# Attention projection of the last stage as three f32r products of high and low parts, with other shares of it moved into the aggregation stage

## The reference, cut to what matters

```
xn = layernorm(x)
x1 = x + gnn(xn, edges) @ W_up + linear_attention(xn) @ Wo + bo
out = x1 + ffn_fp4(layernorm(x1))        # gate, up, silu, down, each operand quantised
```

## Time and profile before

| | us |
|---|---|
| median of 3 runs (lowest, highest) | 1060.36 (1056.84, 1062.06) |
| the profiled execution | 1058.53 |
| its span in the trace | 1056.8 |
| aggregation (about 611 to 816) | 205 |
| last stage (816.2 to the end) | 240.6 |

### The profile page before, as it was taken

How to read it: one execution, slowest core, us unless ns; L and a number is a source line. 1 busy time by engine, 2 the same in 40 slices (tenths; PEclk the granted TensorE clock), 3 DMA queues, 4 the chain that set the end, 5 groups by cost and what they waited for, 6 DMA issues and landing times. The chain is left out here.

```text
span 1056.8 us, 17499 instructions
## 1 busy us (share of the span) xinstructions
PE 959.5 (91%) x5429; PEld 794.3 (75%) x5429; DVE 837.9 (79%) x1395; ACT 648.7 (61%) x1435; POOL 496.7 (47%) x582
## 2 busy tenths in 40 slices
PE   2698879999999999999997779999999879999986
PEld 2676779999999999999997357888898334454443
DVE  5875567888888888888888868998995768887776
ACT  3274446665765766666664568999898335554442
POOL 0211777777777777777771524444444200110000
PEclk9699889999999999999998899999999989999998
DMA  9304588989889898998872689989985364674314
GB/s 246 56 7 110 169 243 259 292 265 280 257 254 294 266 287 284 288 280 282 277 244 91 247 198 332 293 278 310 290 270 192 79 135 122 149 160 112 81 19 79
DMA packets 109977, 221.40 MB, mean 209 GB/s; under 512 B 25883, under 2 KB 58228, under 8 KB 109857
## 3 DMA queue, kind: packets, MB, share of 16 engines
q1 hardware_dynamic: 89053, 159.98, 47.2%
q0 software_dynamic: 20576, 60.08, 23.8%
q10 hardware_dynamic: 260, 0.20, 0.1%
HBM read 156.56 MB, written 62.95 MB: 208 GB/s over the span
## 5 line engine op out<-in xcount | busy, mean ns | idle before, releaser
L1024 POOL DMA_INDIRECT score_gath<-xl_rows,misc x324 | 347.4, 1072 | 101.6 <-issue 92.1
L1064 PE MATMUL score_ps_m<-x_hi,score_w_hi 128*128 128x416 f32 (+1 forms) x576 | 209.4, 363 | 2.1 <-DVE score_w_lo L1217 1.9
L1065 PE MATMUL score_ps_m<-x_lo,score_w_hi 128*128 128x416 f32 (+1 forms) x576 | 204.1, 354 | 0.0
L1066 PE MATMUL score_ps_m<-x_hi,score_w_lo 128*128 128x416 f32 (+1 forms) x576 | 204.1, 354 | 0.0
L1784 ACT ACTIVATE agg_gath<-agg_gath,prob 128x64 f32<-128x64 f32 x648 | 159.2, 353 | 6.7 <-DMA agg_gath<-edge_rows 6.4
L1196 DVE TENSOR_TENSOR score_zb<-score_gath,score_ps_x 128x1024 f32<-128x1024 f32 x81 | 98.8, 1219 | 67.6 <-PE score_ps_x L1047 57.9
L1733 PE MATMUL ps_all<-agg_gath,agg_hot 128*125 128x128 f32 x648 | 128.0, 280 | 9.8 <-DVE agg_hot L1839 6.4
L1735 PE MATMUL ps_all<-agg_gath,agg_hot 128*125 128x136 f32 x648 | 128.9, 281 | 0.0
L1733 PEld LDWEIGHTS ps_all<-agg_gath,agg_hot 128*125 128x125 f32 x648 | 100.5, 189 | 25.8 <-issue 25.2
L2081 PE MATMUL ps_all<-mix_w,phi_c 128*125 128x512 f32 x240 | 108.4, 602 | 5.8 <-DVEq L2355 5.2
L1064 PEld LDWEIGHTS score_ps_m<-x_hi,score_w_hi 128*128 128x128 f32 x576 | 109.7, 190 | 4.2 <-issue 2.6
(11 more groups left out here) (341 smaller groups left out, 1666.3 us busy)
## 6 DMA issues: line engine op xcount, KB each, us to landing
edge_rows<-score_gath SPq DMA_DIRECT2D x81, 528.0 KB, 3.8
agg_gath<-edge_rows SPq DMA_DIRECT2D x81, 528.0 KB, 5.6
local_bc<-local_rows SPq DMA_DIRECT2D x40, 224.0 KB
score_gath<-xl_rows,misc POOLq DMA_INDIRECT x324, 4.5
phi_c<-phi_rows SPq DMA_DIRECT2D x10, 500.0 KB, 6.1
x_bo<-in_x SPq DMA_DIRECT2D x10, 500.0 KB
x_bo<-in_L_mix_bo POOLq DMA_DIRECT2D x10, 500.0 KB, 7.2
out<-fin_x SPq DMA_DIRECT2D x9, 500.0 KB
```

The costliest lines, as they stand in the source:

```text
L1024: nc.gpsimd.indirect_dma_start(out=gath[:, g % GS, q, :], out_offset=None, in_=xl_rows, in_offset=bass.IndirectOffsetOnAxis(ap=src_idx[:, ...
L1064: pe.matmul(acc, w_hi[:, i % 2, kk, :], x_hi[:, kk, cols], start=(kk == 0), stop=False)
L1065: pe.matmul(acc, w_hi[:, i % 2, kk, :], x_lo[:, kk, cols], start=False, stop=False)
L1066: mm = pe.matmul(acc, w_lo[:, i % 2, kk, :], x_hi[:, kk, cols], start=False, stop=(kk == KC - 1))
```

## The change: what it does

The projection in `finish` is no longer f32 times f32. phi and `mix_w` are each split in a high part (rounded to f32r) and a low part (the rest, f32r), and each product becomes three f32r products: high x high, high x low, low x high. ACT makes the high parts (`split_high`, `high_phi`: a copy of 128 x 1024 for each panel, 128 x 750 or 1000 for each chunk), POOL subtracts to get the low parts (`split_low`, `low_phi`), in place over `mix_w` and `phi_c`. Panels 2, 3 and 4 are split by POOL alone during the aggregation, at groups 24, 32 and 40 (a copy and a subtraction each). Panels 5, 6 and 7 follow at the start of `finish`, panels 0 and 1 after `complete_x(2)`. `EARLY` changes from 4, 3, 3, 3, 3, 2, 2 to 8, 2, 2, 2, 2, 2, 2 panels for chunks 0 to 6: chunk 0's projection is done wholly in the aggregation, and `finish` has no `mix_part` for it. Tiles move to other places in memory.

```
-EARLY = [4, 3, 3, 3, 3, 2, 2] + [0] * (NC - 7)
+EARLY = [KC] + [2] * 6 + [0] * (NC - 7)
+PHI_O = 2
+SPLIT = [2, 3, 4, 5, 6, 7, 0, 1]
+SPLIT_EARLY = 3
+def split_low(nc, k, n):
+    kk = SPLIT[n]
+    nc.gpsimd.tensor_tensor(k.mix_lo[:, kk, :], k.mix_w[:, kk, :], k.mix_hi[kk][:, :].bitcast(F32),
+                            ALU.subtract).then_inc(k.s_mix_lo, 1)
...
 # aggregate, POOL
+                def split_early(n):
+                    kk = SPLIT[n]
+                    pool.wait_ge(s_piece, 2)
+                    nc.gpsimd.tensor_copy(k.mix_hi[kk][:, :], k.mix_w[:, kk, :]).then_inc(k.s_mix_hi, 1)
+                    pool.wait_ge(k.s_mix_hi, n + 1)
+                    split_low(nc, k, n)
                 for g in range(NG):
                     extras(g)
+                    for n in range(SPLIT_EARLY):
+                        if g == 24 + 8 * n:
+                            split_early(n)
...
 # finish, POOL
+                def low_phi(c):
+                    part = phi_c[:, c % 2, EARLY[c]:, :]
+                    pool.wait_ge(s_phi_hi, c)
+                    nc.gpsimd.tensor_tensor(phi_lo[:, c % 2, EARLY[c]:, :], part, phi_hi[:, c % 2, EARLY[c]:, :].bitcast(F32),
+                                            ALU.subtract).then_inc(s_phi_lo, 1)
+                low_phi(1)
+                for n in range(SPLIT_EARLY, 6):
+                    pool.wait_ge(k.s_mix_hi, n + 1)
+                    split_low(nc, k, n)
                 pool.wait_ge(k.s_own_in, 16 * 5)
...
                     x_add(nc, k, c, bias_rows(a))
+                    low_phi(c)
...
+                    if c == 0:
+                        for n in range(6, KC):
+                            pool.wait_ge(k.s_mix_hi, n + 1)
+                            split_low(nc, k, n)
...
 # finish, PE
                 def mix_part(c, half):
+                    if half == 0:
+                        pe.wait_ge(s_phi_lo, c)
                     for kk in range(EARLY[c], KC):
-                        pe.matmul(ps_y[0:C, half, :], phi_c[:, c % 2, kk, :], mix_w[:, kk, half * 512:half * 512 + 512],
-                                  start=(kk == EARLY[c]), stop=False)
+                        if half == 0:
+                            pe.wait_ge(k.s_mix_lo, SPLIT.index(kk) + 1)
+                        high, low = phi_hi[:, c % 2, kk, :], phi_lo[:, c % 2, kk, :]
+                        pe.matmul(ps_y[0:C, half, :], high, k.mix_hi[kk][:, cols], start=(kk == EARLY[c]), stop=False)
+                        pe.matmul(ps_y[0:C, half, :], high, k.mix_lo[:, kk, cols], start=False, stop=False)
+                        pe.matmul(ps_y[0:C, half, :], low, k.mix_hi[kk][:, cols], start=False, stop=False)
...
-                pe.wait_ge(s_phi[0], 16)
-                for half in range(2):
-                    mix_part(0, half)
                 turn_gnn(0)
...
 # finish, ACT
+                high_phi(1)
+                split_high(SPLIT_EARLY)
                 act.wait_ge(s_eps, 1)
                 act.wait_ge(s_den, 1)
                 act.activation(node[:, 2:4, :, :], node[:, 2:4, :, :], ACT.Exp).then_inc(s_pself, 1)
+                for n in range(SPLIT_EARLY + 1, 6):
+                    split_high(n)
                 for c in range(4):
                     copy_gnn(c)
...
                 copy_gnn(7)
+                for n in range(6, KC):
+                    split_high(n)
+                high_phi(2)
                 size_x(0)
...
                 normalise(1)
+                high_phi(3)
                 size_x(1)
...
                     gate(c - 1)
+                    if c + 2 < NC:
+                        high_phi(c + 2)
                     size_x(c)
```

More of the change, by code:

```diff
@@ L149, in allocate @@
     k.x_lo = nc.alloc_sbuf_tensor_at("x_lo", [P, KC, N], F32R, offset=x_at + 4 * KC * N)
+    k.mix_at = x_at
     k.mix_w = nc.alloc_sbuf_tensor_at("mix_w", [P, KC, D], F32, offset=x_at)
@@ L182, in allocate @@
     k.kv = sb("kv", [P, PANELS, P])
+    k.kv_at = at(k.kv, 4 * PANELS * P)
     misc = k.misc = sb("misc", [P, HID + 2 * PB * P])
@@ L199, in allocate_late @@
     k.agg_gath = ctx.enter_context(nc.sbuf_tensor("agg_gath", [P, AGG_SLOTS, GP, XW], F32))
+    gath_bytes = 4 * AGG_SLOTS * GP * XW
+    k.gath_at = nc.sbuf_base - gath_bytes
+    assert 4 * D * (KC - SPLIT_EARLY + 1) <= gath_bytes
+    k.s_mix_lo = ctx.enter_context(nc.semaphore("s_mix_lo"))
+    k.s_mix_hi = ctx.enter_context(nc.semaphore("s_mix_hi"))
+    homes = [k.parts_at, k.parts_at + 4 * D, k.kv_at] + [k.gath_at + 4 * D * n for n in range(KC - SPLIT_EARLY)]
+    k.mix_lo = nc.alloc_sbuf_tensor_at("mix_lo", [P, KC, D], F32R, offset=k.mix_at)
+    k.mix_hi = {kk: nc.alloc_sbuf_tensor_at(f"mix_hi{kk}", [P, D], F32R, offset=at) for kk, at in zip(SPLIT, homes)}
     k.prob = ctx.enter_context(nc.sbuf_tensor("prob", [P, PB * P, HEADS], F32))
@@ L210, in allocate_last @@
     k.phi_c = ctx.enter_context(nc.sbuf_tensor("phi_c", [P, 2, KC, C], F32))
+    k.phi_at = nc.sbuf_base - 8 * KC * C
     k.x_bo = ctx.enter_context(nc.sbuf_tensor("x_bo", [C, 2, D], F32))
@@ L1607, in aggregate @@
         hot = sb("hot", [P, OS, GP, C])
-        phi_o = sb("phi_o", [P, 5, 3, C])
+        phi_o = sb("phi_o", [P, 5, PHI_O, C])
         piece = sb("piece", [C, 512])
@@ L1669, in _ @@
                         for c in range(2, 7):
-                            sp.dma_start(phi_o[:, c - 2, :, :], k.phi_rows[0:3, :, C * c:C * c + C].rearrange("k p n -> p k n")).then_inc(s_phi_o, 16)
+                            sp.dma_start(phi_o[:, c - 2, :, :], k.phi_rows[0:PHI_O, :, C * c:C * c + C].rearrange("k p n -> p k n")).then_inc(s_phi_o, 16)
                     if g >= GS + 22 and (g - GS - 22) % 6 == 0 and (g - GS - 22) // 6 < 5:
@@ L1931, in sem @@
             return ctx.enter_context(nc.semaphore("fin_" + name))
-        h = k.kv[0:C, :, :].rearrange("p a b -> p (a b)")
-        square = k.parts[0:C, 0:D]
+        h = nc.alloc_sbuf_tensor_at("fin_h", [C, D], F32, offset=k.gath_at + 4 * D * (KC - SPLIT_EARLY))[:, :]
+        phi_hi = nc.alloc_sbuf_tensor_at("fin_phi_hi", [P, 2, KC, C], F32R, offset=k.parts_at + 8 * D)
+        phi_lo = nc.alloc_sbuf_tensor_at("fin_phi_lo", [P, 2, KC, C], F32R, offset=k.phi_at)
+        square = k.parts[0:C, 4 * D + D // 2:5 * D + D // 2]
         work = k.score[:, :, :].rearrange("p i h -> p (i h)")
-        coarse = k.parts[:, 3 * D:3 * D + D // 2].bitcast(BF16)
+        coarse = k.parts[:, 4 * D:4 * D + D // 2].bitcast(BF16)
         x1 = sb("x1", [C, 3, D])
@@ L1996, in finish @@
         s_tail = sem("s_tail")
+        s_phi_hi = sem("s_phi_hi")
+        s_phi_lo = sem("s_phi_lo")
         s_pself = sem("s_pself")
@@ L2079, in mix_part @@
                 def mix_part(c, half):
+                    cols = slice(half * 512, half * 512 + 512)
+                    if half == 0:
+                        pe.wait_ge(s_phi_lo, c)
                     for kk in range(EARLY[c], KC):
-                        pe.matmul(ps_y[0:C, half, :], phi_c[:, c % 2, kk, :], mix_w[:, kk, half * 512:half * 512 + 512],
-                                  start=(kk == EARLY[c]), stop=False)
+                        if half == 0:
[4 more added lines that the diff above has]
+                        pe.matmul(ps_y[0:C, half, :], low, k.mix_hi[kk][:, cols], start=False, stop=False)
                 def gnn_part(c, half):
@@ L2086, in gnn_part @@
                         m = pe.matmul(ps_y[0:C, half, :], gnn_t[:, kk, C * c:C * c + C], w_up[:, kk, half * 512:half * 512 + 512],
-                                      start=False, stop=(kk == 1))
+                                      start=(kk == 0 and EARLY[c] == KC), stop=(kk == 1))
                     if half:
@@ L2092, in projections @@
                     pe.wait_ge(s_x1, c)
-                    pe.wait_ge(s_phi[c % 2], 16 * (c // 2 + 1))
+                    mix_part(c, 0)
                     pe.wait_ge(s_gtc, c + 1)
-                    mix_part(c, 0)
                     if c in (1, 2):
@@ L2242, in _, with high_phi, split_high @@
                 act.activation(tail[:, :], ps_all[0:C, 5, 0:2 * HALF + UPPER], ACT.Copy).then_inc(s_tail, 1)
+                def high_phi(c):
+                    act.wait_ge(s_phi[c % 2], 16 * (c // 2 + 1))
+                    act.activation(phi_hi[:, c % 2, EARLY[c]:, :], phi_c[:, c % 2, EARLY[c]:, :], ACT.Copy).then_inc(s_phi_hi, 1)
+                def split_high(n):
+                    act.activation(k.mix_hi[SPLIT[n]][:, :], mix_w[:, SPLIT[n], :], ACT.Copy).then_inc(k.s_mix_hi, 1)
+                high_phi(1)
+                split_high(SPLIT_EARLY)
                 act.wait_ge(s_eps, 1)
```

## The result

The changed kernel takes 1080.49 us (median of 4 runs, 1079.93 to 1084.82), the kernel before beside it 1058.69 (4 runs, 1056.84 to 1062.06). The ratio is 1.0205, with a 95% interval of 1.0162 to 1.0248: slower by 22 us, inside the range, 3.5 us above the number forecast. The profiled execution took 1080.66 us, its span is 1078.9.

The account below looks back on a forecast made before the run. PE, ACT and DVE nearly full in the aggregation; in the last stage hand-overs, then DVE, then PE from 907.45. Terms 1.5 + 9.0 + 8.7 - 0.3 + 3.7 - 3.6 = +19.0 on 1058.5, said as 1077 us; range 1056 to 1088.

Parts of the forecast that it names:

- The mechanism: Each new POOL operation holds DVE operations with two SBUF inputs for its whole length, 1.9 to 2.55 us; chance 0.66.
- Rival 1: POOL does not hold DVE anywhere, so the kernel gets faster by 6 us, 1052 us; chance 0.12.
- Rival 2: POOL's hold on DVE never passes 0.52 us, ten times on 1052: 1057 us, the same; chance 0.08.
- The aggregation: POOL adds 11 us against DVE, partly taken by DVE's lead over PE: +1.5 us, bounds -2 and +8.
- rival 3: Aggregation takes POOL's 11 us nearly in full because DVE has no lead there: 1084 us; chance 0.14.
- Start and residual(1): Last stage: POOL's subtractions, ACT's high parts and PE's clock delay residual(0) by 9.0 us, then residual(1) by 8.7.
- the line through the earlier trace: POOL subtraction price from records of 256 and 384 columns: 2.55 us for 1024 columns, bounds 2.1 and 2.95.
- The clock's part: Start of last stage: PE, idle since the aggregation, loses 2.3 us on chunk 0's products at the lower clock level.
- ACT's 2.9: Before `size_x(0)`, on the way to residual(1): two `split_high` and `high_phi(2)` on ACT add 2.9 us.
- Iterations: After residual(2), POOL's `low_phi` makes DVE's 18.85 us 20.7, or 21.3 for 1000 columns: +3.7, then -3.6 us.
- ACT's `high_phi`: Iterations from 907.45 us: its cost counted as nothing; without that cover 0.8 to 1 us a chunk.
- The f32r products: Projection on PE: 0.232 us per 512-column product, bounds 0.19 and 0.232; period 20.5 us for chunks 7 to 9.

Follow-up runs that it names:

- experiment 6: Changed kernel with POOL's nine subtractions for phi's low part replaced by writes of zeros of the same shape: 1072.95 us, ratio 1.0152 to the kernel before.
- experiment 5: Changed kernel with the aggregation's three POOL subtractions cut to one column, its three copies kept whole: 1076.03 us, ratio 1.0165 to the kernel before.
- experiment 3: Kernel before with only the new shares of early panels (8, 2, 2, 2, 2, 2, 2), in f32, nothing split: 1063.64 us, ratio 1.0057.
- experiment 2: Changed kernel with only the aggregation's six POOL copies and subtractions cut to one column: 1072.52 us, ratio 1.0142 to the kernel before.
- experiment 1: Changed kernel with all its new POOL subtractions and copies cut to one column, PE and ACT work the same: 1053.17 us, ratio 0.995 to the kernel before.
- experiment 8: Same split as the change, but 16 early panels, ACT's high parts later where possible, every subtraction on POOL: 1069.12 us, ratio 1.0134 to the kernel before.

## Why the prediction was right

**The mechanism.** Right, and shown: POOL's operations hold DVE's, each DVE operation ends just behind POOL's, on both sides of the range of lengths (40 columns and 1024). But the prediction had it for DVE operations of two SBUF inputs alone, the only kind in the earlier trace rows, and in the iterations the operation held was nearly always L1931, which has one. That it is held for POOL's own time as well was not foreseen, so the price of an iteration came out right in part by luck. Rival 1, worked out at 1052, is the kernel with POOL's operations cut (1053). Rival 2, a hold of at most 0.52 us, fell at the first timeline: holds were 1.5 to 2.2 us. The Trainium skill (SBUF — State Buffer, Who interferes with whom) agrees with the rows: two SBUF inputs on DVE against a GpSimd read exclude each other for the whole instruction, and a GpSimd instruction that only writes does not hold them (0.20 and 0.19 us beside the write of experiment 6).

**The aggregation.** The step that failed: "DVE's lead over PE takes part of it", for which +1.5 was taken, with a bound of +8. It measured +9.2, beyond the bound. There was no lead to take it: six DVE operations are 8.8 us too long and PE's wait for `agg_hot` grows by 6.1. This is the mechanism of rival 3, which was given 0.14; its condition ("DVE has no lead there") held. The copy counts as well, 0.8 us each on DVE's records; with the copies alone 4.2 us of the aggregation stay (experiment 5). That the moved products cost nothing there was right (experiment 3: 206.05 against 205.9).

**Start and residual(1).** Right in kind, 1.0 and 1.6 us too long. A subtraction of 1024 columns made DVE's operations 2.0 to 2.2 us longer, not the 2.55 of the line through the earlier trace rows; POOL's records of 2.7 hold waits. The clock's part, 2.3 us for `gnn_part(0)`, measured 1.35 (4.80 against 3.45), and 1.1 to 2.6 in the other executions, so the 1.0 too long at the start is within what one execution differs from the next: with the same start residual(0) came 21.1 and 20.4 us into the stage in experiments 2 and 5. ACT's 2.9 measured 2.6.

**Iterations.** 20.7 was forecast and 20.5 measured for 750 columns, 21.3 and 20.9 to 21.35 for 1000. The five intervals from residual(4) were forecast at 105.1 and took 103.2, mostly because the last took 19.2 us and not PE's 20.5: no subtraction is left beside it. One reading in this step was wrong: 105.1 was set against 108.68, counted from 907.45, while the two iterations before had been counted to residual(4), at 908.57. Against the 107.57 us from there the step's own prices give -2.5 and not -3.6 (measured -4.3), and the sum is 1.1 higher. ACT's `high_phi` was put at nothing, and rightly: with POOL's operations cut the iterations are 18.9 us (experiment 1).

**The sum.** +19.0 forecast, +22.1 measured between the two profiled executions: 7.7 us too little in the aggregation, 3.1 too much in the last stage (4.2 without the slip of 1.1), and 1.5 that is the difference of two executions. The number came out near because these errors have opposite signs: that is luck.

**The f32r products.** 0.23 us at 512 columns, the upper of the two bounds, and 20.5 us for a chunk on PE: right (experiment 1's last iterations).

## What to carry to other kernels

Work given to an idle POOL isn't free where DVE is busy: as long as POOL reads SBUF, a DVE operation of two SBUF inputs stands still, and here the f32 TENSOR_SCALAR of one input did too. The price on DVE's path is about POOL's own time, larger here than DVE's time for the same work (2.0 against 1.22 us for 1024 columns). So price such work on DVE itself first, put it where DVE waits, and only then ask what POOL could take. Where three engines are over 92% busy, count a hold there in full unless a row shows the lead that would swallow it.

## What the runs showed of the hardware

- A held pair takes turns: DVE's two operations at residual(1) last 3.25 us each, 2.01 of POOL and 1.24 of their own. POOL waits as well, so the mean of its records (2703 ns for 1024 columns) is not its price.
- DVE doesn't always get in between two POOL operations: in experiment 6 one DVE operation lasted 6.35 us beside two subtractions in a row (4.96 us), and ended 1.09 us after the second.
- A POOL copy of 1024 columns holds DVE too (0.8 us more on a DVE record beside each of three), a POOL write of 750 columns doesn't hold an operation of two inputs. Nor did a subtraction hold an operation of 1024 columns with one input in SBUF and the other in PSUM: residual(1) took its usual 1.22 us beside one in experiment 8.
- A DVE operation with one input, TENSOR_SCALAR in f32, is held by a subtraction as well: 2.25 us for 40 columns in experiment 6, and 2.18 against 0.69 in the iteration above. A POOL write holds it too (1.01 against 0.69, ending 0.55 us after the write).
